# Merging the last layer with the last norm, and clearing semaphores inside the next norm, in an eight-stage network on one core

## The chip, the cores and the metric

The kernel runs on one NeuronCore of one Trainium2 chip. The metric is the device time of one execution in microseconds (us). It has the engines TensorE (PE, with weight loads shown apart as PEld), VectorE (DVE), ScalarE (ACT), GpSimd (POOL) and SyncE (SP, which here only starts DMAs).

## The reference

A batch of 4 sequences of 512 tokens with 128 channels passes through four layers. Each layer is a mixer and a feed-forward part, each added to its input and followed by a layer norm without weights: attention with ALiBi and a gated MLP; a selective scan and a mixture of 8 experts; a softmax attention over heads and a mixture of 32 experts with 16 adapters; rotary attention and a feed-forward part in which experts choose tokens. The last of these is what the change touches most:

```python
# expert choice, T = 2048 tokens, 8 experts, 2*T (token, expert) pairs kept over all
scores = softmax(x @ Wr)                       # T x 8
gates  = scores where among the 2*T greatest, else 0
y = (gelu(x @ Ws1 + bs1) @ Ws2 + bs2)          # shared expert
for e in range(8):
    y += gates[:, e:e+1] * (gelu(x @ W1[e] + b1[e]) @ W2[e] + b2[e])
out = layernorm(x + y)
```

## The kernel before

The activations stay in SBUF as `xT`, 128 channels by 2048 tokens, and everything works on batches `i` of 512 columns (`cols(i)`). `network` (L3055) runs eight stages one after the other, then a last norm and the store: a0 (attention), f0 (gated MLP), s (scan), m (mixture of 8), q (softmax attention), x (mixture of 32), a3 (attention), c (expert choice). All stages but a0 and q begin with `layernorm_stage` (L87): per batch two matmuls on PE (L116, L112), Square, Ln and Exp on ACT (L126, L130, L135) and a product on DVE (L162). While it runs, SP issues the loads of the stage's weights.

Stage q (L1661) loads its weights (L1726) at its own start; PE, DVE and ACT wait for them. Stage x routes tokens, then `sparse_experts` (L2275) handles 32 experts in 16 groups of two: POOL fetches each expert's 80 rows by an indirect DMA (L2339) into a ring of 8 buffers, PE transposes and multiplies (L2369, L2384, L2398, L2400), ACT and DVE make SiLU and the gated product (L2437, L2482), DVE computes weights and places for four experts at a time (L2465 to L2474), ACT scales the result (L2429) and POOL scatters it (L2347). POOL's list is: 8 fetches, then fetch e+8 and scatter e in turn.

Stage c is `choice_stage` (L2512), in two blocks after its norm. `choice_route` (L2550) computes logits (L2641), softmax, and the threshold by a search of 16 steps: each step DVE compares (L2715, L2720), PE sums over partitions (L2616), DVE decides (L2724 to L2730). Between these sums PE runs the shared expert (L2622, L2629), ACT its Gelu (L2670). Then come ranks (L2650 to L2757) and the gates, which PE transposes (L2655), DVE copies (L2769) and ACT casts (L2682). `choice_experts` (L2774) first loads `b2` and `select` (L2799), then runs 32 units (4 batches by 8 experts) in a hardware loop over batches. For unit n PE computes four up-products (L2812), a product that spreads the gate (L2814) and, one unit later, four down-products (L2822; with L2825 once a batch); ACT makes the Gelus (L2843), DVE multiplies by the gate (L2853) and, once a batch, adds the result to `xT` (L2857). An fp32 product is two PE instructions (passes) in the trace. After that come c's clears, the last norm over all four batches, a nop and a barrier, and one store of 1 MB (L3096).

## Time and profile before

| | |
|---|---|
| median of 3 runs | 1896.82 us (1896.57 to 1897.28) |
| profiled execution | 1899.36 us, of it span in the trace 1897.6 us |
| busy in the span | PE 81%, DVE 55%, ACT 49%, POOL 22% |
| mean granted TensorE clock | 0.903 of full speed |
| a0 and its clears | 0 to 330.0 us |
| f0 with norm | 330.0 to 513.8 us |
| s with norm | 515.1 to 821.5 us |
| m with norm | 825.4 to 917.7 us |
| q | 919.5 to 1090.0 us |
| x with norm | 1092.0 to 1291.2 us (expert part from 1194.9) |
| a3 with norm | 1296.0 to 1554.3 us |
| c with norm | 1558.1 to 1878.6 us (routing to 1639.8, experts from 1641.1) |
| last norm and store | 1881.3 to 1897.6 us |

The stages follow each other without overlap, so each stretch of the table stands on the path. "Busy" counts neither waits nor semaphore, register or DMA-issuing instructions: clears and nops are seen only as gaps between rows of the timeline. Idle time in square brackets at the end of a row is that engine's own, with what ended it; `PEq L78`, `L70` and `L95` are the ends of blocks (L78 the clears, L70 a barrier after nops, L95 a norm).

### The profile page before, as it was taken

How to read it: one execution, taken by the hardware profiler on the slowest of the kernel's cores; microseconds unless marked ns; L12 is line 12 of the kernel's file. 1: busy time of each engine (PE TensorE's matmuls, PEld its weight loads, DVE VectorE, ACT ScalarE, POOL GpSimd, SP SyncE). 2: the span in 40 equal slices, each digit the busy share in tenths (PEclk: the TensorE clock that was granted, in tenths of full speed). 3: DMA queues.
4: the chain of work that ended last, by engine and by line, in shares of the span. 5: the costliest groups of instructions: out<-in, count | busy, mean ns of one | idle time of the engine just before them, and what ended most of it. 6: DMA issues, size and time to landing. Idle time of an engine off the chain costs nothing. (4 is left out here: it accounts for less than half of the span.)

```text
span 1897.6 us, 22237 instructions
## 1 busy us (share of the span) xinstructions
PE 1541.0 (81%) x7296; PEld 664.5 (35%) x7296; DVE 1039.2 (55%) x2156; ACT 924.2 (49%) x1578; POOL 411.2 (22%) x370
## 2 busy tenths in 40 slices
PE   4699998899848898779799870674899977699997
PEld 1244443343302333234233430672122223344443
DVE  8577772100006999947577649423888825433332
ACT  4766665432257887520166640222477762234343
POOL 4101100000027898700022200560121100000000
PEclk7799998999958999989799985796699997899999
DMA  5112200100000000000111091013121102000000
GB/s 141 43 33 54 60 19 7 56 0 0 19 9 1 5 5 5 1 30 1 35 29 40 1 361 46 18 21 126 59 69 60 35 21 85 6 1 0 0 0 22
DMA packets 51965, 72.21 MB, mean 38 GB/s; under 512 B 11442, under 2 KB 44490, under 8 KB 50103
## 3 DMA queue, kind: packets, MB, share of 16 engines
q1 hardware_dynamic: 49814, 69.20, 12.0%
q0 software_dynamic: 2048, 1.73, 0.5%
q8 instruction: 54, 0.88, 0.2%
q14 instruction: 49, 0.39, 0.1%
HBM read 48.29 MB, written 18.12 MB: 35 GB/s over the span
## 5 line engine op out<-in xcount | busy, mean ns | idle before, releaser
L656 ACT ACTIVATE a_probs_sb<-a_t_ps 128x512 f32<-128x512 f32 x512 | 286.7, 596 | 129.3 <-PE a_t_ps L537 72.8
L747 DVE CUSTOM_DVE_ANT_0 a_biased<-a_s_ps,a_bias 128x512 f32<-128x512 f32 x256 | 166.2, 686 | 67.8 <-issue 67.6
L533 PE MATMUL a_t_ps<-a_stack 126*128 126x512 bf16 (+1 forms) x512 | 169.6, 395 | 30.4 <-DMA a_stack<-a_least_parts 11.7
L514 PE MATMUL a_s_ps<-a_stack 96*128 96x512 bf16 (+1 forms) x512 | 155.4, 412 | 39.4 <-DMA a_stack<-a_stacks 25.3
L1429 DVE TENSOR_TENSOR_SCAN s_h<-s_dA,s_dbu 128x1024 f32<-128x1024 f32 x64 | 146.6, 2290 | 52.9 <-POOL s_dbu L1394 44.3
L754 DVE TENSOR_REDUCE a_least_sb<-a_s_ps 128x2 f32<-128x1024 f32 x128 | 152.7, 1220 | 34.4 <-PE a_s_ps L514 34.1
L1394 POOL TENSOR_TENSOR s_dbu<-s_du,s_bs 128x1024 f32<-128x1024 f32 x64 | 152.3, 2391 | 29.5 <-DVE s_h L1429 27.9
L2843 ACT ACTIVATE c_hid<-c_up_ps,c_b 128x512 f32<-128x512 f32 x128 | 87.9, 687 | 143.6 <-PE c_up_ps L2812 143.6
L2853 DVE TENSOR_TENSOR c_gated_sb<-c_hid,c_g_ps 128x2048 f32<-128x2048 f32 x32 | 73.2, 2288 | 146.4 <-ACT c_hid L2843 146.4
L552 PE MATMUL a_o_ps<-a_probs_sb,a_vpad 128*16 128x512 f32 x1024 | 138.7, 615 | 0.2 <-ACT a_probs_sb L656 0.2
L2812 PE MATMUL c_up_ps<-xT,c_w 128*128 x256 | 118.0, 605 | 6.0 <-DMA c_select<-in_c_select 6.0
L1234 PE MATMUL s_y_ps<-s_hc,ident 128*128 128x512 f32 x256 | 121.1, 595 | 1.3 <-DVE s_hc L1436 1.3
L2822 PE MATMUL c_y_ps<-c_gated_sb,c_w 128*128 128x512 f32 x256 | 115.1, 592 | 0.0
L1827 ACT ACTIVATE q_probs_sb<-q_s_ps,q_most_sb 128x512 f32<-128x512 f32 x128 | 86.6, 683 | 45.8 <-DVE q_most_sb L1905 45.0
L514 PEld LDWEIGHTS a_s_ps<-a_stack 96*128 96x128 bf16 (+1 forms) x512 | 37.8, 97 | 176.5 <-DVE a_least_sb L747 59.3
L1329 ACT ACTIVATE s_dA<-s_delta,s_decay 128x1022 f32<-128x1022 f32 x64 | 71.4, 1115 | 56.0 <-DVE s_h L1429 54.4
L1905 DVE TENSOR_REDUCE q_most_sb<-q_s_ps 128x2 f32<-128x1024 f32 x64 | 77.4, 1222 | 27.1 <-PE q_s_ps L1773 27.1
L537 PE MATMUL a_t_ps<-a_steps,a_slopes_diag 128*128 128x128 bf16 x768 | 85.4, 220 | 0.0
L537 PEld LDWEIGHTS a_t_ps<-a_steps,a_slopes_diag 128*128 128x128 bf16 x768 | 65.1, 98 | 55.2 <-issue 2.2
L1436 DVE TENSOR_TENSOR s_hc<-s_c_ps,s_h 128x1024 f32<-128x1024 f32 x64 | 78.4, 1224 | 8.4 <-PE s_c_ps L1222 6.3
L841 POOL CAST a_least_parts<-a_least_turned 16x128 bf16<-16x128 f32 x32 | 8.9, 280 | 322.9 <-ACT a_least_turned L650 322.9
L2812 PEld LDWEIGHTS c_up_ps<-xT,c_w 128*128 128x128 f32 x256 | 49.7, 195 | 68.3 <-issue 67.9
(452 smaller groups left out, 2539.9 us busy)
## 6 DMA issues: line engine op xcount, KB each, us to landing
x_wu<-in_x_wu SPq DMA_DIRECT2D x2, 4096.0 KB, 17.9
a_stacks<-a_p SPq DMA_DIRECT2D x16, 384.0 KB, 3.0
a_stack<-a_stacks SPq DMA_DIRECT2D x32, 192.0 KB, 3.9
a_stack<-a_stacks SPq DMA_DIRECT2D x64, 96.0 KB, 2.3
a_stacks<-a_p SPq DMA_DIRECT2D x16, 256.0 KB, 2.4
q_q<-q_q SPq DMA_DIRECT2D x32, 128.0 KB, 2.3
x_wd<-in_x_wd SPq DMA_DIRECT2D x2, 2048.0 KB, 33.5
c_w<-in_c_w SPq DMA_DIRECT2D x2, 2048.0 KB, 10.6
```

What stands on the lines that cost most here:

```text
L514: made = nc.tensor.matmul(s_ps[:, 2 * (x % 2) + e, :], operand(0, k, pair, e, SCORE_ROWS)[:, t * P:(t + 1) * P], operand(1, k, pair, e, SC ...
L533: last = nc.tensor.matmul(out, operand(1, k, pair, e, TURNED_ROWS)[:, t * P:(t + 1) * P], operand(0, k, pair, e, TURNED_ROWS), start=True, ...
L537: last = nc.tensor.matmul(out[:, t * P:(t + 1) * P], slopes_diag[:, r, h, :], steps_table[:, :], start=False, stop=(r == 2))
L552: last = nc.tensor.matmul(o_ps[h * VPAD:h * VPAD + VWIDE, :], vpad[:, i % 2, t, g * GROUP + h, :], probs[:, y % PROB_RING, h % 2, :], star ...
L656: nc.scalar.activation(probs[:, y % PROB_RING, e, :], bank("turned", y, e), ACT.Exp, scale=-1.0).then_inc(probs_ready, 1)
L747: nc.vector.tensor_tensor_reduce(out=biased[:, e, :], in0=s_ps[:, 2 * (x % 2) + e, :], in1=bias[:, h, at:at + N], scale=1.0, scalar=3.0e38 ...
L754: nc.vector.tensor_reduce(least[:, k % 2, both], s_ps[:, 2 * (x % 2):2 * (x % 2) + 2, :], axis=AX.X, op=ALU.min).then_inc(least_ready, 1)
L1234: last = nc.tensor.matmul(y_ps[:, :], core.ident[:, :], hc[:, p % 2, r, :], start=False, stop=(n == STATES - 1 and r == BRANCHES - 1))
L1394: nc.gpsimd.tensor_tensor(dbu[:, p % IN_RING, :, :], du[:, i % 2, :, :], bs[:, p % B_RING, :, :], ALU.mult).then_inc(input_ready, 1)
L1429: nc.vector.tensor_tensor_scan(h[:, k % 2, :, :].rearrange("p r t -> p (r t)"), dA[:, :, :].rearrange("p r t -> p (r t)"), dbu[:, k % IN_R ...
L2812: nc.tensor.matmul(up_ps[u % RING][:, :], w1[:, e, m * P:(m + 1) * P], xT[:, cols(i)], start=True, stop=True).then_inc(up_ready, 1)
L2822: last = nc.tensor.matmul(y_ps[:, :], w2[:, e, k, :], gated[:, e % 2, k, :], start=(e == 0 and k == 0), stop=(e == E - 1 and k == CH_HT - 1))
```

## The change

- No semaphore starts at 1 any more, so the nops and their barriers go; waits for 0 are left out. Only ten semaphores of the expert part of x keep START, and POOL raises these during the routing of x.
- The clearing block of each stage goes. POOL clears a stage's semaphores inside the norm that opens the next stage (q's with m's, in the norm of x), and those of c in the block that ends the program.
- m and q are one stage; q's weights are loaded behind m's during the norm of m.
- f0's hardware loops over batches are written out.
- In the expert part of x each expert has buffers of its own. POOL issues all 32 fetches first (fetch e waits until fetch e-4 has landed), then all 32 scatters. ACT and DVE run hardware loops over turns of two groups, with computed waits and addresses; PE's list is written out. Weights and places are computed per group of two experts.
- c after its norm is one block. The load order is changed; the up-products and Gelus of unit 0 stand before the search; the rank products stand after the first of the shared expert's last four down-products; up-products run three units ahead (4 buffers, gated in place); gates are transposed, copied and cast batch by batch between the units. Each batch is normed and stored while the next is made, the last one in two halves of 256 columns.

The core of the diff:

```diff
-    def run_stage(self, stage, *args):
-        self.stage_sems = []
-        with ExitStack() as self.stage_ctx:
-            stage(self, *args)
-            with self.nc.Block() as block:
-                @block.gpsimd
-                def _(pool):
-                    for handle in self.stage_sems:
-                        pool.sem_clear(handle)
+    def clear_stale(self, pool):
+        for handle in self.stale_flags:
+            pool.sem_clear(handle)
+        self.stale_flags = []
...
 def layernorm_stage(core, xT, tag, out=None, prefetch=None, wide_range=False):
+        @block.gpsimd
+        def _(pool):
+            core.clear_stale(pool)
...
 def moe_and_query_stage(core, A, xT):
+                sp.dma_start(wd[:, :, :], A["m_wd"]).then_inc(w_loaded, 16)
+                query.load(sp, A)
...
 def sparse_experts(...):
             def fetch(e):
-                if e >= X_RING:
-                    pool.wait_ge(turned, (e - X_RING) // PAIR + 1)
-                    pool.wait_ge(weighed, (e - X_RING) // SOME + 1)
+                if e >= SOME:
+                    pool.wait_ge(fetched[e % SOME], 16 * (e // SOME))
...
-            for e in range(X_RING):
+            for e in range(E):
                 fetch(e)
             for e in range(E):
-                if e + X_RING < E:
-                    fetch(e + X_RING)
                 scatter(e)
+        def run(engine, body):
+            body(0)
+            with engine.Fori(1, TURNS - 1) as i:
+                body(i)
+            body(TURNS - 1)
...
 def choice(core, xT, W, loaded, shared_loaded, first_loaded, w_loaded, out):
+            wait(pe, first_loaded, 32)
+            up(0)
+            wait(pe, shared_loaded, 48)
+            for i in range(B):
+                for m in range(CH_HT):
+                    count_all(CH_HT * i + m)
+                    shared_up(i, m)
+                    if i > 0:
+                        shared_down(i - 1, m)
+            count_all(SEARCH_STEPS)
+            shared_down(B - 1, 0)
+            wait(pe, equal_ready, 1)
...
+            wait(pe, w_loaded, 64)
+            for n in range(1, AHEAD):
+                up(n)
+            turn_gates(0)
+            up(AHEAD)
+            spread_gates(0)
+            turn_gates(1)
+            turn_gates(2)
+            for n in range(UNITS):
+                if n + 1 < UNITS:
+                    spread_gates(n + 1)
+                if n > 0 and n + AHEAD < UNITS:
+                    up(n + AHEAD)
+                if n == 1:
+                    turn_gates(3)
+                if n % E == 0 and n > 0:
+                    centre(n // E - 1)
+                if n % E == 1 and n > E:
+                    variance(n // E - 1)
+                down(n)
+            centre(B - 1)
+            centre(B)
+            variance(B - 1)
+            variance(B)
...
         def _(act):
+            for n in range(UNITS):
+                if n > 0 and n + AHEAD < UNITS:
+                    gelus(n + AHEAD)
+                if 1 <= n < B:
+                    cast_gates(n)
+                if n % E == 0 and n > 0:
+                    squares(n // E - 1)
+                if n % E == 1 and n > E:
+                    nc.scalar.preload_act_table_set("natural_log_exp_and_others")
+                    root(n // E - 1)
...
 def network(nc, A, out):
-        for stage, _ in STAGES:
-            core.run_stage(stage, A, xT)
-        layernorm_stage(core, xT, "last_ln")
-        stored = core.sem("out_stored")
+        ctx.enter_context(core.run_stages(STAGES, A, xT))
         with core.block() as block:
             @block.sync
             def _(sp):
-                sp.dma_start(out, xT[:, :]).then_inc(stored, 16)
-                sp.wait_ge(stored, START + 16)
+                sp.wait_ge(core.stored, 16 * len(LAST_PIECES))
+            @block.gpsimd
+            def _(pool):
+                core.clear_stale(pool)
```

## Rows read from the trace of the kernel before

**Rows 1.** Timeline, ends of stages f0, q, x (start us, us, engine, line, operation, [idle before])

```profile
513.05 0.75 DVE L1012 SCALAR_TENSOR_TENSOR xT<-f_hid_ps,f_scales,xT 128x512 f32<-128x512 f32 x1 [33.42 <-PE f_hid_ps L953]
515.11 1.28 ACT L139 ACT_TABLE_LOAD   x1 [5.85 <-PEq L78]
...
1089.51 0.48 DVE L1895 SCALAR_TENSOR_TENSOR xT<-q_o_ps,q_mask,xT 128x256 f32<-128x256 f32 x1
1092.01 1.28 ACT L149 ACT_TABLE_LOAD   x1 [6.46 <-PEq L78]
...
1290.51 0.69 DVE L2498 TENSOR_TENSOR xT<-x_t_ps,xT 128x512 f32<-128x512 f32 x1 [0.57 <-PE x_t_ps L2416]
1296.03 1.28 ACT L149 ACT_TABLE_LOAD   x1 [19.66 <-PEq L78]
```

**Rows 2.** Timeline, a change of block without clears, and the one before c's routing

```profile
1104.59 2.90 DVE L2186 TENSOR_SCALAR x_small_sb<-xT 128x2048 f32<-128x2048 f32 x1 [0.30 <-PEq L95]
...
1568.75 0.69 DVE L162 TENSOR_TENSOR xT<-c_ln_ps_centred,c_ln_rs 128x512 f32<-128x512 f32 x1 [0.63 <-ACT c_ln_rs L135]
1571.54 6.91 PE L2641 MATMUL c_logits_ps<-c_wr,xT 128*128 128x8 f32 x32 [4.21 <-PEq L70]
```

**Rows 3.** Timeline, start of stage q

```profile
919.52 1.28 ACT L1817 ACT_TABLE_LOAD   x1 [26.80 <-PEq L78]
923.59 2.07 PE L1738 MATMUL q_p_ps<-xT,avg 128*128 128x512 f32 x2 [6.62 <-DMA q_mask<-in_q_mask]
```

**Rows 4.** Timeline, PE, first four passes of the norms of s and of m

```profile
515.15 1.96 PE L116 MATMUL s_ln_ps_centred<-xT,centre 128*128 128x512 f32 x4 [2.13 <-PEq L78]
825.44 3.75 PE L116 MATMUL m_ln_ps_centred<-xT,centre 128*128 128x512 f32 x4 [6.00 <-PEq L78]
```

**Rows 5.** Timeline, expert part of x: first fetch, two groups, last group, last scatter

```profile
1195.74 1.12 POOL L2339 DMA_INDIRECT x_got<-x_rows,x_fetch_at  x1 [88.11 <-issue]
...
1212.44 0.71 PE L2384 MATMUL x_up_ps<-x_slotsT,x_wau 128*128 128x160 f32 x4
...
1216.27 0.71 PE L2384 MATMUL x_up_ps<-x_slotsT,x_wau 128*128 128x160 f32 x4
...
1271.23 0.71 PE L2384 MATMUL x_up_ps<-x_slotsT,x_wau 128*128 128x160 f32 x4
...
1276.01 0.36 ACT L2429 ACTIVATE x_results_sb<-x_d_ps,x_weight 80x128 f32<-80x128 f32 x1 [0.53 <-PE x_d_ps L2400]
...
1277.54 0.91 POOL L2347 DMA_INDIRECT x_results<-x_results_sb,x_put_at  x1 [0.30 <-issue]
```

**Rows 6.** Timeline, the search's hardware loop on DVE

```profile
1583.34 0.16 DVE L2715 TENSOR_TENSOR c_trial<-c_threshold_sb,c_bits 128x3 int32<-128x3 int32 x1 [0.39 <-DVE c_threshold_sb L2730]
...
1585.03 0.21 DVE L2727 TENSOR_SCALAR c_growth<-c_enough,c_unit 128x1 int32<-128x1 f32 x1 [0.15 <-DVE c_is_enough L2724]
```

**Rows 7.** Timeline, c: first sum of the search, after the search, last products

```profile
1582.02 0.17 PE L2616 MATMUL c_total_ps<-c_count_sb,c_ones_b 128*128 128x3 bf16 x1 [3.56 <-DVE c_scratch L2720]
...
1624.48 3.67 PE L2629 MATMUL c_shared_y_ps<-c_shared_hid,c_w 128*128 128x512 f32 x8 [1.43 <-ACT c_kept L2662]
...
1628.71 0.29 DVE L2740 COPY c_totals<-c_places_ps 128x128 f32<-128x128 f32 x1 [5.43 <-PE c_places_ps L2650]
...
1634.43 0.28 DVE L2765 TENSOR_TENSOR c_gate_parts<-c_scores,c_middle 128x128 f32<-128x128 f32 x1
...
1870.68 7.03 PE L2822 MATMUL c_y_ps<-c_gated_sb,c_w 128*128 128x512 f32 x16
...
```

**Rows 8.** Timeline, ACT, a change of function table in f0

```profile
412.27 1.28 ACT L973 ACT_TABLE_LOAD   x1 [1.09 <-PE f_up_ps L932]
413.57 1.26 ACT L973 ACTIVATE f_silu_sb<-f_up_ps,f_scales 128x512 f32<-128x512 f32 x2
```

**Rows 9.** Timeline, ACT, a step of the last norm; the DMA view, a load of 128 KB

```profile
1891.35 0.63 ACT L135 ACTIVATE last_ln_rs<-last_ln_lv 128x512 f32<-128x512 f32 x1
...
m_wg<-in_m_wg SPq DMA_DIRECT2D x1, 128.0 KB, 2.1
```

More of the change, by code:

```diff
@@ L21 @@
 LN_EPS = 1e-5
-START = 1
 def cols(i, size=N):
@@ L955, in second_and_out @@
                 last.then_inc(out_ready, 1)
[L957 removed]
+            wait(pe, w_loaded, 32)
             up(0)
[L959 to L960 removed]
+            wait(pe, hidden_loaded, 32)
+            for i in range(B - 1):
                 first(i)
@@ L1015, in _ @@
             gate(0)
-            with dve.Fori(0, B - 1) as i:
+            for i in range(B - 1):
                 gate(i + 1)
@@ L2403, in _ @@
-            turn(0)
-            pe.wait_ge(w_loaded, 16 * 8)
-            for n in range(len(UNITS_ALL) + 1):
-                if n < len(UNITS_ALL):
-                    up(n)
-                    g, e = UNITS_ALL[n]
-                    if e is None and g + 1 < G:
-                        turn(g + 1)
-                if n:
-                    down(n - 1)
+                nc.tensor.matmul(out, hid[:, u - kind, (kind - 1) * CAP:kind * CAP], one(wad, g),
+                                 start=False, stop=True).then_inc(down_ready, 1)
@@ new lines, in experts @@
+            def experts(i):
+                for u in range(UNITS):
+                    up(i, u)
+                    if u == 0:
+                        turn(i, 1)
+                    if u == PAIR + 1 and not (isinstance(i, int) and i == TURNS - 1):
+                        turn(i + 1, 0)
+                    if u > 0:
+                        down(i, u - 1)
+                    elif not (isinstance(i, int) and i == 0):
+                        down(i - 1, UNITS - 1)
+            turn(0, 0)
@@ L2413, in _ @@
+            pe.wait_ge(w_loaded, 16 * 8)
+            for i in range(TURNS):
+                experts(i)
+            down(TURNS - 1, UNITS - 1)
             for i in range(B):
@@ new lines, in result, with experts @@
+                wait(act, down_ready, e + 1)
+                wait(act, weighed, g + 1)
+                nc.scalar.activation(one(results, e), d_ps[kind - 1][0:CAP, 0:C], ACT.Copy,
+                                     scale=weight[:, 0, PAIR * a + kind - 1:PAIR * a + kind]).then_inc(result_ready, 1)
+            def experts(i):
+                for u in range(UNITS):
+                    n = UNITS * i + u
+                    wait(act, up_ready, n + 1)
+                    wait(act, act_ready, n - 1)
+                    nc.scalar.activation(silu[:, u % 2, :], up_ps[u % 3][:, 0:PAIR * CAP], ACT.Silu) \
+                        .then_inc(silu_ready, 1)
+                    if u >= 2:
+                        result(i, u - 2)
+                    elif not (isinstance(i, int) and i == 0):
+                        result(i - 1, UNITS + u - 2)
@@ L2490, in _ @@
+            keep(0, 0)
+            run(dve, experts)
             for i in range(B):
@@ new lines, in wait_up_bank, with _ @@
+        def wait_up_bank(engine, use):
+            last = use - UP_BANKS
+            if last < 0:
+                return
+            if last < UPS_BEFORE:
+                wait(engine, gelu_ready, last + 1)
+            elif last < UPS_BEFORE + CH_HT * B:
+                wait(engine, shared_gelu_ready, last - UPS_BEFORE + 1)
+            else:
+                wait(engine, gelu_ready, last - CH_HT * B + 1)
+        @block.sync
+        def _(sp):
+            for p in range(len(LAST_PIECES)):
+                wait(sp, normed, p + 1)
+                sp.dma_start(out[:, piece(p)], xT[:, piece(p)]).then_inc(core.stored, 16)
@@ new lines, in down @@
+            def down(n):
+                i, e = divmod(n, E)
+                wait(pe, gated_ready, n + 1)
+                if n == 0:
+                    wait(pe, y_copied, B)
+                if e == 0:
+                    wait(pe, added, i)
+                for k in range(CH_HT):
+                    last = nc.tensor.matmul(y_ps[:, :], w2[:, e, k, :], hid[:, n % HID_RING, k, :],
+                                            start=(e == 0 and k == 0), stop=(e == E - 1 and k == CH_HT - 1))
+                    if e == 0 and k == 0:
+                        nc.tensor.matmul(y_ps[:, :], b2[:, :], gates[:, cols(i)], start=False, stop=False)
+                last.then_inc(down_ready, 1)
@@ L2640, in _ @@
+            wait(pe, loaded, 16 * 6)
             for t in range(TT):
@@ new lines, in normalise @@
+            def normalise(p):
+                wait(dve, rstd_ready, p + 1)
+                nc.vector.tensor_tensor(xT[:, piece(p)], norm_banks(p)[0], of_batch(rstd, p),
+                                        ALU.mult).then_inc(normed, 1)
+            copy_gates(0)
+            gate(0)
+            for n in range(UNITS):
+                if n + 1 < UNITS:
+                    gate(n + 1)
+                if 1 <= n < B:
+                    copy_gates(n)
+                if n % E == 2 and n > E:
+                    normalise(n // E - 1)
+                if n % E == E - 1:
+                    add(n // E)
```

820 lines of the change are left out of this document (416 added, 404 removed).

## The prediction

> **What bounds the kernel now.** Read the stretches in the table first: the stages follow each other without overlap, so every gap between them is on the path. Then the timeline round each gap. f0's last product ends at 513.80 and s begins at 515.11; q ends at 1089.99, x begins at 1092.01; x ends at 1291.20, a3 begins at 1296.03 [rows 1]. So 1.31, 2.02 and 4.83 us for 11, 21 and 61 clears: a straight line, (4.83 - 1.31)/50 = 0.0704 us per clear on 0.54 us, which is two changes of block, each 0.28 to 0.30 [rows 2]. Inside the stages PE is the bound where passes stand back to back at 0.43 us (8 passes in 3.67, 16 in 7.03, [rows 7]). In the expert part of x it is POOL: 64 indirect DMAs, each 0.91 behind 0.30 of issue, between 1195.74 and 1278.45 [rows 5]. Before the search of c it is a chain of short steps, and the end is a row of things that wait for each other: last product, clears, norm, store.
>
> **Clears.** 46+11+47+14+21+61+39 = 239 leave the path: 239 x 0.0704 = 16.8. In the norms POOL has nothing else, and a norm takes over 10 us against at most 4.3 us of clears (61), so I cost them there at nothing; without that cover they would cost the same again. Seven blocks go with them, 7 x 0.27 = 1.9. Together **18.7**. c's 30 are counted at the end.
>
> **Nops and barriers.** Before c's routing, DVE ends at 1569.44 and PE begins at 1571.54, 2.10 [rows 2]; less a plain change of 0.28 that is 1.8 for 20 nops and one barrier: 0.07 each, as for a clear, and 0.4. On the path stand 6 (start), 11 (f0), 3 (c's norm), 20 (routing): 40 x 0.07 + 4 x 0.4 = **4.4**. The change to c's routing stays as a plain one. The 7 before c's experts and the last one are in the sums for c and the end.
>
> **q's weights.** q begins at 919.52, its PE waits for `q_mask` until 923.59 [rows 3]. With the load behind m's, 90 us earlier, these **4.1** go. SP's queue only issues q's loads after m's own, so m's don't come later. After it, the wait is for nothing loaded.
>
> **TensorE's clock.** s's first four norm passes took 1.96 after 2.13 of idleness, m's 3.75 after 6.00 [rows 4]: 0.43 and 0.85 a pass, that is 2.4 and 1.2 GHz. With shorter gaps PE is idle less before m, c and q, so fewer passes run at the low level: 1.8 in m, some 0.8 in c, 1.0 in q. I take **3.5**; bounds 0 (the level falls just the same) and 6 (x, a3 and a0's successor gain too).
>
> **f0's loops written out.** The edge of an iteration shows no gap of PE that a written list would close; the nearest price of a loop step is 0.39 of idleness in front of L2715, of a computed address 0.15 at L2727 [rows 6], and f0 has three such edges, off or on the path. 0 to 1, take **0**.
>
> **Expert part of x.** The fetches and scatters are 64 x (0.91 + 0.30) = 77.8 if POOL never waits, against 82.7: 4.9 is waiting. After the change fetch e waits for the landing of fetch e-4, 4.8 us earlier in the list, so seldom; all 32 are issued in 38.9 us. The groups of two experts go at 3.83 us when not held back (first product 1212.44 to 1216.27, third and fourth of 16), so the sixteenth begins at 1212.44 + 13 x 3.83 = 1262.2. A last group ends its results 5.1 after that product (1271.23 to 1276.37): 1267.3 [rows 5]. The last scatter begins at 1195.74 + 77.8 - 0.9 = 1272.6. So POOL stays the bound by 5.2 us, which is 0.33 per group. I take **4.5** of the 4.9, for a late fetch or two. ACT and DVE get hardware loops and about 29 computed operands per group; at [rows 6] prices of 0.03 to 0.34 that is 1 to 10 us a group spread over two engines, mostly beside PE. This is the largest unknown, taken up under the rivals.
>
> **c to the last product.** The up-products of unit 0, 8 passes, go ahead of the search. They cost 8 x 0.43 to 8 x 0.85 = 3.4 to 6.8, but the first sum stands at 1582.02 behind 3.56 of waiting [rows 7], so the search moves by 0 to 3.3; take 2.0 lost. Steps of the search stay as they are: PE's sums come between products as now. The search's end: rank products stand behind one down-product, not four, so behind 0.86 of the 3.67 us at 1624.48. Their copy on DVE, now 1628.71, comes at 1626.1, 2.6 earlier, and so the gates, now ready at 1634.71, at 1632.1 [rows 7]. PE meanwhile does three down-products (2.6) and up(1), up(2) (6.8), until 1635.4, then the first transpose, up(3), the spread and two more transposes, until 1641.6, and waits for the first gating; down(0) begins at about 1642.5. What is left for PE from there: 264 down and bias passes x 0.427 = 112.8; 28 units' up-products, 224 x 0.427 = 95.7; 30 spreads x 0.21 = 6.3; the last transpose 0.9; 12 norm passes 5.1; sum 220.8. The norms between units change ACT's table three times there and back. In f0 a load of 1.28 is followed 0.02 later by the ACTIVATE [rows 8]; the Gelus run three units ahead, so PE feels 0.5 each, 1.5. That makes 1642.5 + 222.3 = 1864.8, against 1870.68 + 7.03 = 1877.7 now: 12.9, less the 2.0: **11.0**. Stalls go from the load of `b2` and `select` and from the turn of each batch; late next is DVE, whose gating of a unit is shorter than PE's 6.9 us per unit.
>
> A rule speaks against this part. The Trainium skill, "ScalarE: Activation LUTs", section "What ACT_TABLE_LOAD costs", has some 1.38 us of drain beside each load's 1.28. Row [rows 8] has none behind the load. By the rule each switch would stall PE some 1.4 us more, the sum would be 4.1 us higher.
>
> **The end.** Now 1877.7 to 1897.6: 19.9. Afterwards three batches are normed and stored already, and the last one in halves. From the last product: DVE's addition of a half (0.48, as the 128x256 row in [rows 1]), centring, squares, variance, logarithm and exponential (ACT 0.63 for 512 columns, [rows 9]), product, second half one step behind: product done at +4.4, issue +0.4, and a store of 128 KB is 2.1 from issue [rows 9], so it lands at about +6.9. In parallel to the landing come a change of block and 38 clears, 0.27 + 2.7, of which 2.3 beside the landing of the store (2.1 and its wait stand in the same last block): 4.75 + 0.27 + 2.7 + 0.2 = 7.9 in all. Saved **12.0**.
>
> **Sum.** 18.7 + 4.4 + 4.1 + 3.5 + 0 + 4.5 + 11.0 + 12.0 = 58.2. The profiled execution took 1899.4, so 1841.2; the median of the runs lies 2.5 under it: **1839**. The unknowns give -6 to +9: clock +-3, first up-product +-1.5, x from -0.4 to several, end +-2.
>
> **Rivals.** (A) The hardware loops make ACT or DVE the bound in x. A step of 4.6 instead of 3.83, by two loop-like prices of 0.39, gives 16 x 0.77 = 12.3, of which 5.2 is covered: +7, **1846**. For it: many computed operands; against: most of them can run while PE has its 3.83 us of products.
> (B) The clears are not free inside the norms, because work of the other engines waits for POOL's list, and a block still costs what it did: 16.8 + 1.9 back, **1858**. For it: nothing; against: the norms are longer than the clears.
> (C) A change of function table holds ACT for twice its load: 3 x 1.28 = +3.8, **1843**. For it, no row here; against, [rows 8]. The page named above speaks for it.
> (D) Slower: computed waits and addresses stand on the chain of each group in x, 14 of the 29 at 0.34. The group becomes 3.83 + 4.8 = 8.6, +76 - 5, **1910**. It decides from a group of about 7.7 us: (7.7 - 3.83) x 16 - 5 = 57, all that the rest gains. For it: the 0.39 of [rows 6]; against: the 0.15 there is for an address, and most stand off the chain.
> (E) The change of order in c or the norms between units do not overlap: per batch 4 us of norm exposed, three times, +12, **1851**.
>
> **How the numbers follow.** Forecast, within 6 us of 1839: 0.70. A 0.12, B 0.06, C 0.05, D 0.02, E 0.05. The range takes the forecast with its unknowns, A, C and E: 1830 to 1854. A measurement of this kernel tells 0.2%, about 4 us; no case but D comes near 1897. Faster 0.97, same 0.01, slower 0.02.
>
> **What would show it.** Gaps between stages near 0.3, seven of them; POOL's clears nowhere in a gap. q's first product directly on the block change. Passes of 0.43 in m's norm. Fetches of x in one row of 39 us, then scatters at 1.21 spacing without idleness; if they are idle with ACT or DVE named, A or D. In c, PE at 6.9 per unit with at most 0.5 more at a norm; the last store issued about 5 us behind the last product. Wrong is the forecast if x with its norm takes over 197 us (now 199.2), or c from its first logits to the end over 307 (now 326).

## The result and the profile after

The changed kernel takes 1827.82 us in the median (1826.27 to 1828.75, 4 runs) beside 1897.05 us before: ratio 0.9634, 95% interval 0.9618 to 0.9651. The forecast of 1839 us had the direction right and was 11 us too high, just below its range (1830 to 1854). The profiled execution has a span of 1825.8 us against 1897.6, so there are 71.8 us to account for.

Read the ends of the stages first. This is the timeline of the changed kernel (start us, us, engine, line, operation, in brackets the engine's idle time before it and what ended it), at the ends of f0, m, q, x and in front of c's routing, where [rows 1 to 3] stood:

```profile
500.81 0.75 DVE L1010 SCALAR_TENSOR_TENSOR xT<-f_hid_ps,f_scales,xT 128x512 f32<-128x512 f32 x1 [33.41 <-PE f_hid_ps L951]
501.84 1.28 ACT L137 ACT_TABLE_LOAD   x1 [4.83 <-PEq L899]
...
894.09 0.69 DVE L1641 TENSOR_TENSOR xT<-m_t_ps,xT 128x512 f32<-128x512 f32 x1 [0.42 <-PE m_t_ps L1542]
895.10 2.04 PE L1749 MATMUL q_p_ps<-xT,avg 128*128 128x512 f32 x2 [1.05 <-PEq L1492]
...
1253.59 0.69 DVE L2526 TENSOR_TENSOR xT<-x_t_ps,xT 128x512 f32<-128x512 f32 x1 [0.58 <-PE x_t_ps L2436]
1254.55 1.28 ACT L147 ACT_TABLE_LOAD   x1 [14.73 <-PEq L2309]
...
1522.83 0.69 DVE L160 TENSOR_TENSOR xT<-c_ln_ps_centred,c_ln_rs 128x512 f32<-128x512 f32 x1 [0.64 <-ACT c_ln_rs L133]
1523.82 5.00 PE L2776 MATMUL c_r_ps<-c_wr,xT 128*128 128x8 f32 x32 [2.41 <-PEq L89]
```

Every gap is now 0.27 to 0.31 us: 0.28 behind f0 (it was 1.31), 0.27 behind x (4.83), 0.30 before the routing (2.10). PE of q begins 0.32 after the end of m; it no longer waits for a load. The next block shows TensorE at the start of a norm, that of m and that of a3, to be held against [rows 4]:

```profile
806.93 1.96 PE L114 MATMUL m_ln_ps_centred<-xT,centre 128*128 128x512 f32 x4 [2.42 <-PEq L1040]
...
1254.58 3.75 PE L114 MATMUL a_ln_ps_centred<-xT,centre 128*128 128x512 f32 x4 [1.03 <-PEq L2309]
```

In m the four passes that took 3.75 us take 1.96: the granted clock is 2.4 GHz instead of 1.2. In a3 they still take 3.75, although PE was idle for only 1.03 us. That row is the first sign that the idle gap alone does not set the clock.

In f0, which the forecast had put at 0, DVE's additions came at this distance in the kernel before:

```profile
395.59 0.75 DVE L1012 SCALAR_TENSOR_TENSOR xT<-f_hid_ps,f_scales,xT 128x512 f32 x1 [16.86 <-PE f_hid_ps L953]
437.24 0.75 DVE L1012 SCALAR_TENSOR_TENSOR xT<-f_hid_ps,f_scales,xT 128x512 f32 x1 [16.85 <-PE f_hid_ps L953]
```

In the changed kernel the timeline of DVE and ACT shows this:

```profile
385.88 0.75 DVE L1010 SCALAR_TENSOR_TENSOR xT<-f_hid_ps,f_scales,xT 128x512 f32<-128x512 f32 x1 [16.74 <-PE f_hid_ps L951]
...
401.49 1.28 ACT L971 ACT_TABLE_LOAD   x1
...
426.26 0.75 DVE L1010 SCALAR_TENSOR_TENSOR xT<-f_hid_ps,f_scales,xT 128x512 f32<-128x512 f32 x1 [16.74 <-PE f_hid_ps L951]
```

A batch takes 40.38 us from one addition to the next, where it took 41.65. The load of the table for SiLU has no bracket: ACT did not stand idle before it. In [rows 8] the same load had "1.09 <-PE f_up_ps" in front of it.

The expert part of x (first fetch, two groups, last scatter; compare [rows 5]):

```profile
1164.00 1.12 POOL L2353 DMA_INDIRECT x_got<-x_rows,x_fetch_at  x1 [87.48 <-issue]
...
1201.36 0.71 PE L2396 MATMUL x_up_ps<-x_slotsT,x_wau 128*128 128x160 f32 x4
...
1205.40 0.71 PE L2396 MATMUL x_up_ps<-x_slotsT,x_wau 128*128 128x160 f32 x4
...
1240.78 0.91 POOL L2361 DMA_INDIRECT x_results<-x_results_sb,x_put_at  x1 [0.30 <-issue]
```

POOL's 64 DMAs end after 77.7 us (82.7 before), at 1.215 us each and without a wait. And c, from the first down-product to the end, with the change of function table between units (compare [rows 7, 9]):

```profile
1593.48 1.13 PE L2755 MATMUL c_y_ps<-c_hid,c_w 128*128 128x512 f32 x2 [1.28 <-DVE c_hid L2980]
...
1661.30 1.28 ACT L2879 ACT_TABLE_LOAD   x1
1662.59 0.69 ACT L2845 ACTIVATE c_lv<-c_r_ps,eps 128x512 f32<-128x512 f32 x1
...
1708.07 0.75 DVE L2986 SCALAR_TENSOR_TENSOR xT<-c_y_ps,c_bs,c_kept 128x512 f32<-128x512 f32 x1 [4.58 <-PE c_y_ps L2755]
...
1768.01 0.75 DVE L2986 SCALAR_TENSOR_TENSOR xT<-c_y_ps,c_bs,c_kept 128x512 f32<-128x512 f32 x1 [4.58 <-PE c_y_ps L2755]
...
1810.36 7.03 PE L2755 MATMUL c_y_ps<-c_hid,c_w 128*128 128x512 f32 x16
...
1821.64 0.42 DVE L2991 TENSOR_TENSOR xT<-c_up_ps,c_rs 128x256 f32<-128x256 f32 x1 [0.39 <-ACT c_rs L2850]
```

The last product ends at 1817.39, 8.4 us ahead of the end (19.9 before). A batch of eight units with a norm in it takes 59.94 us (1708.07 to 1768.01).

The account, in us of the two spans, each from the rows above or the same rows of the timeline of before:

| term | forecast | measured |
|---|---|---|
| gaps, nops, barriers (eight gaps 24.65 to 2.32, start 0.57) | 23.1 | 22.9 |
| q's weights | 4.1 | 4.1 |
| TensorE's clock and small shifts (a0 0.4, f0 2.9, s 1.7, m 4.4, x 1.7, a3 1.3, c's norm -0.3) | 3.5 | 12.1 |
| f0's loops | 0 | 3.8 |
| expert part of x | 4.5 | 5.0 |
| c from first logits to last product (306.2 to 293.6) | 11.0 | 12.6 |
| the end (19.9 to 8.4) | 12.0 | 11.5 |
| sum | 58.2 | 72.0 |

The terms add up to the 71.8 of the spans within rounding. Two of them carry the miss: the clock (8.6) and f0 (3.8). The sum is short by 13.8 us and the forecast by only 11, because it took off 2.5 us more for the median lying under the profiled execution, and after the change the two are the same (1827.82 and 1827.58).

Is the 12.1 really clock? The clock records of the two traces say that most of it is. TensorE stood at the lower level for 362 us of the span before and for 290 us after, and its passes ran in about 184 and 142 us of that. By stage the passes at the lower level took 20.3 and 19.9 us in a0, 9.1 and 3.4 in f0, 29.4 and 27.8 in s, 15.8 and 6.2 in m, 24.7 and 18.5 in x, 41.8 and 38.9 in a3 (q: no change). A pass takes twice as long there (0.85 against 0.43), so half of each difference is what the clock can have given: as an estimate 13 us in these stages together, beside the 12.1 measured. In s only 0.8 of the 1.7 is explained so. The same records show 28.8 and 16.4 us in c and 3.4 and 0 at the end, so the terms of c and of the end hold some clock too, up to 6 and 1.7 us.

### The profile page after: what moved, and what is told of

Its sections match the earlier page's. It is cut to its first block and busy times, and to the rows that moved or that the text cites. A ratio compares the mean times of both kernels' runs of the same rounds, so it can differ in the third digit from the quotient of the medians.

```text
span 1825.8 us, 21817 instructions
## 1 busy us (share of the span) xinstructions
PE 1521.9 (83%) x7300; PEld 653.2 (36%) x7300; DVE 1046.1 (57%) x2214; ACT 930.3 (51%) x1585; POOL 410.6 (22%) x370
## 5 line engine op out<-in xcount | busy, mean ns | idle before, releaser
L2980 DVE TENSOR_TENSOR c_hid<-c_hid,c_g_ps 128x2048 f32<-128x2048 f32 x32 | 73.1, 2286 | 132.3 <-PE c_g_ps L2744 132.3
L2726 PE MATMUL c_up_ps<-xT,c_w 128*128 128x512 f32 x256 | 117.9, 602 | 1.2 <-ACT c_hid L2830 1.2
L2755 PE MATMUL c_y_ps<-c_hid,c_w 128*128 128x512 f32 x256 | 115.7, 592 | 1.3 <-DVE c_hid L2980 1.3
L531 PEld LDWEIGHTS a_t_ps<-a_stack 126*128 126x128 bf16 (+1 forms) x512 | 43.8, 97 | 82.6 <-ACT a_probs_sb L654 48.2
```

Source lines behind the costliest of these rows:

```text
L531: last = nc.tensor.matmul(out, operand(1, k, pair, e, TURNED_ROWS)[:, t * P:(t + 1) * P], operand(0, k, pair, e, TURNED_ROWS), start=True, ...
L2726: nc.tensor.matmul(up_ps[up_use(n, m) % UP_BANKS][:, :], w1[:, e, m * P:(m + 1) * P], xT[:, cols(i)], start=True, stop=True).then_inc(up_r ...
L2755: last = nc.tensor.matmul(y_ps[:, :], w2[:, e, k, :], hid[:, n % HID_RING, k, :], start=(e == 0 and k == 0), stop=(e == E - 1 and k == CH_ ...
```

## The experiments

Twelve kernels ran, in three series of four. In the first series the kernel before took 1918.12 us (1911.75 to 1926.7), in the other two 1898.85 and 1897.98. The first and the third have the same chip number, the second another, so the 20 us belong to the series and not for certain to a chip. Between series, only ratios to the kernel before and distances within a trace are compared.

**f_written and f_early_load: what gained in f0.** The first writes out the three loops:

```diff
-            with pe.Fori(0, B - 1) as i:
+            for i in range(B - 1):
                 first(i)
-            with act.Fori(0, B - 1) as i:
+            for i in range(B - 1):
-            with dve.Fori(0, B - 1) as i:
+            for i in range(B - 1):
```

> The kernel before with the three hardware loops of f0 (PE, ACT, DVE) written out and nothing else changed. Theory (a load of the function table): in the loop ACT loads the table for SiLU only once PE's up-product is there; written out, the load follows the Gelu before it and runs beside PE's products. That takes one load of 1.28 us per batch out of the chain, three times: 3.8 us less, 1893.2, and the distance from one addition to xT to the next falls from 41.65 to about 40.4 us. Rival (price of a loop step, as forecast): 0 to 1 us less, the table load still waits for PE.

The second keeps them:

```diff
                 gelu1(i)
+                nc.scalar.preload_act_table_set("silu_and_others")
                 silus(i + 1)
```

> The kernel before with its hardware loops kept; ACT is told to load the table for SiLU right after the first Gelus of each iteration, ahead of the wait for the up-product. Theory (table load): the same 3.8 us less as with the loops written out. Rival (the loops themselves cost the 1.27 us a batch): no change, 1897.

In f_written DVE's first two additions start at 393.72 and 434.10. The timeline of f_early_load, the same two and ACT's load:

```profile
395.02 0.75 DVE L1013 SCALAR_TENSOR_TENSOR xT<-f_hid_ps,f_scales,xT 128x512 f32 x1 [16.85 <-PE f_hid_ps L953]
...
410.63 1.28 ACT L994 ACT_TABLE_LOAD   x1
...
435.60 0.75 DVE L1013 SCALAR_TENSOR_TENSOR xT<-f_hid_ps,f_scales,xT 128x512 f32 x1 [16.85 <-PE f_hid_ps L953]
```

40.38 us per batch written out, 40.58 with the loops kept and the load moved, 41.65 as it was. So of the 1.27 us, 1.07 is the load and 0.2 the loop. The whole times say the same less sharply in this series: ratio 0.9953 (0.9937 to 0.9970) and 0.9982 (0.9966 to 0.9999), where 3.8 us would be 0.998. That f_written gained more than its f0 shows was not pursued.

**busy_gaps and clears_apart: the clock behind a gap.** busy_gaps leaves every clearing block of the kernel before at its length and gives PE products to do in it:

```diff
+                @block.tensor
+                def _(pe):
+                    for _ in range(len(self.stage_sems) // 6):
+                        self.nc.tensor.matmul(idle_ps[:, :], self.idle[:, 0:P], self.idle[:, :], start=True, stop=True)
```

> The kernel before with every clearing block kept at its length, but PE runs bf16 products on a tile of its own in it (one for every six clears: 7, 1, 7, 2, 3, 10, 6, 5). Output and clears are unchanged. Theory (idle PE lowers its clock, and the passes behind the gap pay): the first passes after the gaps stay at 0.43 us, worth 4.4 us in m, 2.9 in f0, 1.8 in x and 1 to 3 in a3 and c: 8 to 12 us less in all, about 1887. Rival (the clock does not depend on the gap, or PE was idle too long already ahead of the clears): within 2 us of 1897.

Ratio 0.9937 (0.9908 to 0.9966), about 12 us less (6.5 to 17.6 by the interval), with nothing taken off the path. This is the view of one tile, the passes of m's norm (ns shortest/median/longest, first and last start), for busy_gaps:

```profile
L122 PE MATMUL m_ln_ps_centred<-xT,centre x8: 592/592/667, 821.2 to 826.2; 128*128 128x512 f32 x8
```

and for f_written, which has the gaps of before and ran in the same series:

```profile
L116 PE MATMUL m_ln_ps_centred<-xT,centre x8: 592/1061/1192, 820.1 to 828.0; 128*128 128x512 f32 x8
```

The median pass falls from 1061 ns to 592. From first norm pass to first product behind the norm, m takes 10.2 us instead of 13.1, f0 10.3 instead of 12.8, a3 10.2 instead of 12.4, x 11.1 instead of 11.6, c 13.5 instead of 13.4. That is 7.9 us in sum, and from c's last product to the last normalised batch it is 13.5 instead of 15.0. In c the first four passes stay at the lower level although PE had products in the gap; why, is open. Elsewhere the clock is a real price of what stands idle before a norm.

clears_apart is the reverse, on the changed kernel:

```diff
             stale_ctx, self.stale_flags = self.stage_ctx, self.stage_flags
+            if stage is not stages[-1]:
+                with self.nc.Block() as block:
+                    @block.gpsimd
+                    def _(pool):
+                        self.clear_stale(pool)
```

> The changed kernel with the clears put back into a block of their own behind each stage (m and q remain one stage, so six such blocks and 239 clears less none). Theory: 239 x 0.0704 + 6 x 0.27 = 18.4 us for the gaps, and another 8 to 12 us because the clock of PE falls in them again, so 27 to 30 us more than 1827.8, about 1856. Rival (the gaps alone): 18.4 more, 1846. Rival (clears in the norm cost as much as outside it): no change.

Ratio 0.9807 (0.9781 to 0.9833), which in this series is 1883.67 us. PE's idle times in front of the six norms grew from 8.17 to 26.43 us in sum, by 18.3, as the price of a clear has it. Nor are the norms longer for the clears in them: m's takes 10.2 us in the changed kernel, with the clears of s in it, and 10.2 in busy_gaps, without. So the clears in the norms are free, and the rival that they are not is out. The norms themselves grew by only 2.3 us in sum (f0, m and x by 0.9 to 1.3, a3 fell by 1.0), and all stretches outside the gaps and the expert part of x by 5.1 us, not by 8 to 12: half of my expectation fell. The rest of the time, 33.4 us, is something else, seen in ACT's timeline of this kernel in the expert part of x:

```profile
1207.18 0.30 ACT L2462 ACTIVATE x_silu_sb<-x_up_ps 128x160 f32<-128x160 f32 x1 [12.44 <-remote]
...
1228.23 0.30 ACT L2462 ACTIVATE x_silu_sb<-x_up_ps 128x160 f32<-128x160 f32 x1 [20.49 <-remote]
```

ACT stood still twice, while its operands were there and POOL issued fetches back to back. The last scatter came 110 us behind the first fetch, instead of 77.

**changed_again and x_order.** Is that the kernel's or the series'?

> The changed kernel itself, unaltered, so that its neighbours in this series are compared on one chip. On the chip of the first four runs (kernel before 1918 instead of 1897) the expert part of x was longer: ACT stood still for 12 and 20 us between two SiLUs while POOL issued its 32 fetches. Theory (that chip serves ACT's and DVE's code late while indirect DMAs are issued): if this series falls on such a chip, the same two stalls appear here too and the changed kernel gains some 35 us less; if on a chip like the first, 1828 against 1897, with no stall over 1 us between SiLUs. Rival (the stalls came with the clearing blocks of that run): no stall on either.

Ratio 0.9630 (0.9614 to 0.9646), 1827.64 us, no such stall. So it isn't the changed kernel as such. Nor is it a lasting trait of the chip: the third series, with the first one's chip number, shows none either. Its cause stays open, and whether the unaltered changed kernel would have stalled in the first series was not tried. There, the three variants of the kernel before show ACT idle for 3 to 5 us, four to six times each behind the first, at the same line; in before's own profile it never is for 3 us behind the first SiLU.

x_order puts POOL's list back:

```diff
-            for e in range(E):
+            for e in range(8):
                 fetch(e)
             for e in range(E):
+                if e + 8 < E:
+                    fetch(e + 8)
                 scatter(e)
```

> The changed kernel with POOL's list in x as it was before (8 fetches, then fetch e+8 and scatter e in turn), each expert keeping its own buffers. Forecast's reading (the ring of buffers and weights per four made POOL wait, not the order): no change on a chip without stalls, within 1 us, POOL still at 1.215 us per DMA without idleness. Rival (fetching first is what gained): the 4.9 us come back, 1833. On a chip with stalls of ACT: shorter stalls than the two of 12 and 20 us, since fetches are no longer issued back to back, so faster than the changed kernel by 10 to 25 us.

The times are not told apart (ratio 0.9640, 0.9622 to 0.9659), the trace is clear. POOL's timeline of x_order, at the ninth DMA:

```profile
1174.80 0.91 POOL L2353 DMA_INDIRECT x_got<-x_rows,x_fetch_at  x1 [0.30 <-issue]
1179.33 0.95 POOL L2361 DMA_INDIRECT x_results<-x_results_sb,x_put_at  x1 [3.62 <-ACT x_results_sb L2451]
```

The first scatter waits 3.62 us for the first result, with 23 fetches still to come. The part takes 82.8 us again. The gain came from the order, not from taking away the ring: the rival was right.

**x_written: the hardware loops in x.**

```diff
-            body(0)
-            with engine.Fori(1, TURNS - 1) as i:
-                body(i)
-            body(TURNS - 1)
+            for i in range(TURNS):
+                body(i)
```

> The changed kernel with ACT's and DVE's hardware loops over turns in the expert part of x written out (constants for waits and addresses). In the changed kernel a group of two experts takes 4.04 and 4.25 us in turn, against 3.83 before the change. Theory (computed operands and loop steps on the group's chain): groups fall to 3.8 to 3.9 us, the last group begins 3 to 5 us earlier, and the time stays within 1 us, because POOL's 64 indirect DMAs at 1.215 us still end last. Rival (groups go by landing fetches or by PE): 4.1 us as now.

1825.99 us, ratio 0.9617 (0.9596 to 0.9638). PE's timeline of x_written:

```profile
1208.42 0.71 PE L2394 MATMUL x_up_ps<-x_slotsT,x_wau 128*128 128x160 f32 x4
1212.25 0.71 PE L2394 MATMUL x_up_ps<-x_slotsT,x_wau 128*128 128x160 f32 x4
```

3.83 us per group, as for the third and fourth group before the change, and the last group begins 66.3 us behind the first fetch. With the loops it was 70.5 in changed_again: 4.04 and 4.25 in turn. POOL takes 77.7 and 77.8 us. The loops cost 0.3 us a group, and POOL covers it. This is rival A's mechanism at less than half its size.

**first_unit_late and ranks_late: what the order in c was worth.**

```diff
             wait(pe, first_loaded, 32)
-            up(0)
...
-            for n in range(1, AHEAD):
+            for n in range(AHEAD):
                 up(n)
```

> The changed kernel with the up-products and Gelus of unit 0 behind the shared expert, as before the change. Forecast's reading: the first sum of the search comes up to 2.4 us earlier, and PE has 3.4 us more to do between the search and the first gating, where it now waits 1.3: the first down-product comes 2.1 - 2.4 = about 0 later, so -0.5 to +1 us in all. Rival (the passes ahead of the search keep PE's clock high and so pay twice): 2 to 4 us slower.

Ratio 0.9637 (0.9621 to 0.9653), 3 us above changed_again in the median, within the spread. PE's timeline of first_unit_late, before the search and at the first unit:

```profile
1527.60 6.97 PE L2776 MATMUL c_r_ps<-c_wr,xT 128*128 128x8 f32 x32 [2.41 <-PEq L89]
1538.13 0.17 PE L2707 MATMUL c_r_ps<-c_count_sb,c_ones_b 128*128 128x3 bf16 x1 [3.57 <-DVE c_scratch L2922]
...
1601.28 1.13 PE L2755 MATMUL c_y_ps<-c_hid,c_w 128*128 128x512 f32 x2 [1.29 <-DVE c_hid L2978]
```

The first sum comes 10.53 us behind the start of the logits here, and 10.42 in both profiles of the changed kernel. That looks as if unit 0 cost nothing in front of the search. But the logits took 6.97 us here and 4.90 in changed_again: TensorE's clock differs, and hides the price. The neighbour to compare with is x_order, which has unit 0 ahead, the same code in c, and logits of the same 6.97. PE's timeline of x_order:

```profile
1526.81 6.97 PE L2778 MATMUL c_r_ps<-c_wr,xT 128*128 128x8 f32 x32 [2.41 <-PEq L89]
...
1538.77 0.17 PE L2709 MATMUL c_r_ps<-c_count_sb,c_ones_b 128*128 128x3 bf16 x1
...
1597.80 1.13 PE L2757 MATMUL c_y_ps<-c_hid,c_w 128*128 128x512 f32 x2 [1.29 <-DVE c_hid L2982]
```

The first sum comes 11.96 us behind the start of the logits, 1.4 later than in first_unit_late: the eight passes need more than PE's idle 3.57. So the 2.0 us that the forecast took off are there, at 1.4. From the start of the logits to the first down-product it is 70.99 us against 73.68. So having unit 0 first gains 2.7 us in c; beside changed_again it seems to be 4.0, of which the clock has a part. Of the 2.7, 0.7 lies in the search itself: its first pair of passes takes 2.05 us in first_unit_late and 1.10 in x_order, as the rival has it that unit 0 keeps the clock up.

```diff
-            shared_down(B - 1, 0)
+            for m in range(CH_HT):
+                shared_down(B - 1, m)
             wait(pe, equal_ready, 1)
```

> The changed kernel with the rank products behind all four of the shared expert's last down-products, as before the change. Forecast's reading: DVE's copy of the totals and so the gates come 2.6 us later, PE waits for the first gating already, so the first down-product and the end come 2.6 us later (the copy of the totals to the first down-product stays 15.8 us, the last sum of the search to the copy grows from 3.2 to 5.8). Rival (the wait is covered by up-products): no change.

1828.10 us, ratio 0.9632 (0.9614 to 0.9649). DVE's timeline of ranks_late:

```profile
1575.46 0.16 DVE L2941 TENSOR_SCALAR c_needed<-c_r_ps 128x1 f32<-128x1 f32 x1 [0.54 <-PE c_r_ps L2707]
1580.97 0.29 DVE L2943 COPY c_totals<-c_r_ps 128x128 f32<-128x128 f32 x1 [5.35 <-PE c_r_ps L2792]
...
1588.20 0.69 DVE L2973 COPY c_gates<-c_g_ps 96x512 f32<-96x512 f32 x1 [1.22 <-PE c_g_ps L2735]
1591.86 4.48 DVE L2979 TENSOR_TENSOR c_hid<-c_hid,c_g_ps 128x2048 f32<-128x2048 f32 x2 [2.97 <-PE c_g_ps L2744]
```

and of changed_again:

```profile
1574.61 0.16 DVE L2942 TENSOR_SCALAR c_needed<-c_r_ps 128x1 f32<-128x1 f32 x1 [0.54 <-PE c_r_ps L2707]
1577.55 0.29 DVE L2944 COPY c_totals<-c_r_ps 128x128 f32<-128x128 f32 x1 [2.78 <-PE c_r_ps L2791]
...
1587.35 0.69 DVE L2974 COPY c_gates<-c_g_ps 96x512 f32<-96x512 f32 x1 [3.77 <-PE c_g_ps L2735]
1591.01 4.48 DVE L2980 TENSOR_TENSOR c_hid<-c_hid,c_g_ps 128x2048 f32<-128x2048 f32 x2 [2.97 <-PE c_g_ps L2744]
```

The copy of the totals is 2.57 us later behind the last sum, and the first gating is 16.40 us behind it in both. DVE's wait for the turned gates shrinks from 3.77 to 1.22 in exchange: PE gets to the transpose no sooner, since it has up(1) and up(2) to finish. The earlier rank products gain nothing. The expectation read the forecast wrongly there: its own sum ran over PE's list (until 1635.4), which ends behind the gates (1632.1), and had no 2.6 us in it.

**norms_last, busy_tails and busy_norms_last: less than 1828.** norms_last takes the norms out from between the units:

```diff
-                if n % E == 0 and n > 0:
-                    centre(n // E - 1)
-                if n % E == 1 and n > E:
-                    variance(n // E - 1)
                 down(n)
-            centre(B - 1)
-            centre(B)
-            variance(B - 1)
-            variance(B)
+            centre(0)
+            for p in range(B + 1):
+                if p < B:
+                    centre(p + 1)
+                variance(p)
```

> The changed kernel with the norms of all four batches behind the last unit (five pieces in three pairs of banks, buffers for 2048 columns), stores still piece by piece. From the sum: PE has 12 norm passes (5.1 us) and up to 1.5 us of table loads less between units, and the end grows by the norm of three more batches at the 1.7 us per batch of the old last norm plus its table load, 5 to 7 us. So 0 to +2 us in all. Rival (overlapping is worth the whole of what the end lost, 10 us or more): +6 us or more.

1825.24 us, ratio 0.9613 (0.9597 to 0.9629), against 0.9630 of changed_again: not slower, and by the trace a little faster. DVE's timeline of norms_last:

```profile
1704.80 0.75 DVE L2973 SCALAR_TENSOR_TENSOR xT<-c_y_ps,c_bs,c_kept 128x512 f32<-128x512 f32 x1 [4.58 <-PE c_y_ps L2755]
1762.36 0.75 DVE L2973 SCALAR_TENSOR_TENSOR xT<-c_y_ps,c_bs,c_kept 128x512 f32<-128x512 f32 x1 [4.58 <-PE c_y_ps L2755]
...
1819.21 0.42 DVE L2978 TENSOR_TENSOR xT<-c_up_ps,c_rs 128x256 f32<-128x256 f32 x1 [0.47 <-ACT c_rs L2841]
```

57.56 us per batch instead of 59.94 (three times 2.4, 7.2), and 10.3 us instead of 4.7 from last product to last normalised piece: 1.5 us less in sum. Norms between units of a stage that PE bounds move their passes, they do not hide them: of the 11.5 us that the end gained, 5.6 were bought so, for 7.2 between the units. The other 5.9 also come with the norms at the end. The clears, the nop, the higher clock and the stores piece by piece are what differs there; what each is worth was not measured.

busy_tails gives PE bf16 products in the waits that end a0, a3 and x:

```diff
+def stay_busy(core, out, count):
+    for _ in range(count):
+        core.nc.tensor.matmul(out, core.idle[:, 0:P], core.idle[:, :], start=True, stop=True)
...
+                    if k == ALL_GROUPS - 1:
+                        stay_busy(core, s_ps[:, 0, :], 2)
...
+            stay_busy(core, d_ps[0][:, :], 20)
             for i in range(B):
                 pe.wait_ge(mixed, i + 1)
```

> The changed kernel with bf16 products on a tile of their own in PE's waits at the end of a0 and a3 (7 each) and of x (23). Output unchanged. Theory (PE's clock falls in the sparse tail of a stage, and the norm behind pays): the way from the first norm pass to the first product behind the norm falls from 11.7, 12.5 and 11.9 us (f, a3, c) to about 10.3 each, so 4 to 6 us less in all, about 1823. Rival (only waits as long as the former clears lower the clock; the tails do not matter): no change, or slower by the products themselves, up to 2 us.

1823.69 us, ratio 0.9609 (0.9592 to 0.9626). The passes of a3's norm (view of the tile) in busy_tails:

```profile
L119 PE MATMUL a_ln_ps_centred<-xT,centre x8: 592/592/1191, 1254.9 to 1260.4; 128*128 128x512 f32 x8
```

and in changed_again:

```profile
L114 PE MATMUL a_ln_ps_centred<-xT,centre x8: 592/827/1192, 1254.6 to 1261.9; 128*128 128x512 f32 x8
```

From first norm pass to the product behind the norm: f0 10.22 (11.68 in changed_again), a3 10.69 (12.50), c 10.22 (11.70), x 10.22 (11.66). The last of these is not the products' doing: none stands in front of x's norm, and ranks_late, which has none at all, has no slow pass there either (view of the tile in ranks_late):

```profile
L114 PE MATMUL x_ln_ps_centred<-xT,centre x8: 593/593/667, 1064.1 to 1069.1; 128*128 128x512 f32 x8
```

x_written, x_order and first_unit_late have 10.22 in x as well, and the last two in c too. So busy_tails is better held against ranks_late, of the same series: a0 is 1.2 us shorter, f0 0.6, a3 with the gap before it 3.7, while s and q take 0.7 more and c with its norm 1.4 more (its logits take 6.43 us against 5.10, and the first sum comes later). PE was also idle for less in front of the norms (a3 0.30 instead of 1.03, f0 and c 0.47 instead of 1.11), so the products in the tail and the shorter wait are not told apart.

> Both at once: the products of busy_tails and the norms of norms_last, which by its trace had 7.2 us less between units and 5.7 us more at the end. Theory: the gains add, 4 to 6 and 1.5 to 2.4 us less, about 1820. Rival (no gain from the tails): 1825 as norms_last.

1822.27 us (1821.42 to 1823.15), ratio 0.9603 (0.9586 to 0.9620): the fastest of all, 5.4 us below changed_again in the median. Alone the two gained 2.4 and 4.0, so they nearly add. It is also simpler in c than the changed kernel.

## Why the prediction was wrong

- **Clears, nops, barriers: right.** 23.1 forecast, 22.9 measured; the line of 0.0704 us per clear on [rows 1] held, and clears_apart brought 18.3 of 18.4 back.
- **q's weights: right**, 4.1.
- **TensorE's clock: the term that was mis-sized, past its own bound of 6.** "I take 3.5; bounds 0 and 6" was put together from m's first four passes (1.8), c (0.8) and q (1.0). The trace shows 12.1 us in stretches to which no other term applies, and passes at the lower level that can account for about 13 of it. In m alone it was 4.4: the whole norm (12.71 to 10.21) and the products behind it (1.9) run at the higher clock, not only the first four passes. f0's norm and first products gave 2.9, which the step left out, and x 1.7. q gave nothing (its first product 2.07 and 2.04), and c's norm took 0.3 longer. busy_gaps shows by a run of its own that filling the gaps was worth about that much in the kernel before. How much the shorter gaps bring is less sure: with the gaps restored (clears_apart) the stretches outside them grew by 5.1 us, less than half. Where the rest comes from is open. It also lies now here and now there: in x_order, ranks_late and x_written the products of m take 1.8 us more and x's norm 1.5 less than in the changed kernel's profile, in stages that the edits did not touch. 0.9 of the 1.7 of s has no known cause.
- **f0's loops: "The edge of an iteration shows no gap of PE ... take 0" failed.** I looked for the price of the loop at its edge. It lay in the middle, in ACT's table load, which in the loop came behind the wait for PE. [rows 8] says so in its bracket, and I read that row only for the 0.02 us behind the load. 1.27 us per batch, three times, 3.8 in all, of it 1.07 each the load (f_early_load).
- **Expert part of x: the amount right (4.5 against 5.0), the reason half wrong.** Not the ring but the first scatter's place in the list made POOL wait. Groups went at 4.04 to 4.25, not 3.83, hidden as the step's slack of 0.33 per group allowed. The prices of 0.03 to 0.34 per computed operand stand in none of the rows named (they have 0.39 and 0.15); x_written shows 0.28 us per group for all of them.
- **c: near in sum (12.6 against 11.0), by luck in part.** The 2.0 of loss for unit 0 was real: from the end of the logits to the first sum it went from 3.56 to 5.42 us, and at equal logits it was 1.4. It did not show because the logits took 5.00 us instead of 6.91, clock that the step did not count. The first down-product comes 69.7 us behind the start of the logits, where the step had 73.0 with its 2.0; the stretch from there to the last product was 223.9 us against 222.3. What went is above all a wait of which the step speaks in half a sentence, here in PE's timeline of the kernel before:

```profile
1644.41 6.51 PE L2812 MATMUL c_up_ps<-xT,c_w 128*128 x8 [6.00 <-DMA c_select<-in_c_select]
```

The eight passes behind it take 6.51 us instead of some 3.6: the clock was at the lower level for 17.1 us from 1633.0 on. In the changed kernel there is no such stretch.
- **The end: right**, 8.4 us against 7.9, though norms_last shows that having three batches normed already was paid for between the units.
- **Rivals.** A came at less than half its size and covered. B: clears_apart says no. C: 1661.30 + 1.28 = 1662.58, and the ACTIVATE starts at 1662.59. The Trainium skill, "ScalarE: Activation LUTs", section "What ACT_TABLE_LOAD costs", has about 1.38 us of drain beside the load. This trace shows none behind it, and so does not agree there. D did not come. E did not come: the norms cost 2.4 us per batch, and 2.2 of it were in the sum (5.1 for the passes, 1.5 for the tables).

Five terms were right within 2 us, in sum if not in every part, and c's with the help of a clock that it had not reckoned with. The two that failed lay above their stated bounds (6 and 1), and both errors had the same sign, so the range missed too.

## What to carry to other kernels

Read the bracket of a table load: if it waits for another engine, a load issued ahead of that wait gains most of its 1.28 us each time (1.07 here), with the loop kept. When idle gaps in front of dense TensorE work go, look at the passes behind them over the whole stretch, not the first few; idle waits can be filled with products on a tile of their own. Work moved between the units of a stage that its engine bounds is moved, not hidden: norms_last was as fast. When two variants are compared by a distance in a trace, look whether the passes ahead of it ran at the same clock.

## What the runs showed of the hardware

- 41 bf16 products on unused data in the clearing blocks, none on the path, made the kernel before about 12 us (0.6%) faster, and 37 products in tails the changed one 4 us (1823.69 against 1828.10 in ranks_late of the same series). The granted clock was 0.910 instead of 0.901 in f_written, and 0.927 instead of 0.921.
- TensorE ran norm passes at 1.2 GHz after 1.03 us of idleness behind the sparse tail of x, and at 2.4 GHz after 2.42 us behind s.
- The same code behind the same idle time ran at either level: x's norm took 11.70 us in the changed kernel and 10.22 in ranks_late, x_written and x_order, each after 1.39 us of idleness of PE, while the products of m, earlier, took 77.6 and 79.4.
- One series of three served the expert part of x 21 to 33 us slower, with the chip number of another that did not. Its traces show ACT idle at a SiLU for 3 to 20 us with "remote" as the cause, always while indirect DMAs were issued; that ACT waited for its own code fits the label, but was not shown.
